# State space outputs transposed and in pairs of heads, decays in two rounded parts, feed-forward weights rounded transposed

## The reference

```python
zxbcdt = u @ W_in
z, xBC, dt = split(zxbcdt, [1024, 1024 + 1280])
conv = conv_b + sum over 4 taps of shifted xBC * conv_w[i]
x, B, C = split(silu(conv), [1024, 1152])       # 16 heads of 64; state 128
dt = softplus(dt + dt_bias);  A = -exp(A_log)
y, _ = ssd(x * dt, A * dt, B, C)                # y[l] = sum over s <= l of (C[l].B[s]) exp(sum of A dt over s+1..l) x[s] dt[s]
y = (y + x * D) * silu(z)
y = y * rsqrt(mean(y * y) + eps) * norm_scale
out = y @ W_out
# feed-forward, weights and activations rounded to 255 steps per row (scale = max|row| / 127)
gate, up = split(quant(h) @ quant(w_gate_up).T);  out = quant(silu(gate) * up) @ quant(w_down).T
```

## Time and profile before

| | |
|---|---|
| median of 3 runs | 1077.93 us (1075.56 to 1081.33) |
| the profiled execution | 1079.65 us, of which its span (first to last instruction) 1077.9 us |
| busy in the span | PE 95%, DVE 68%, ACT 53%, POOL 25% |
| mean granted TensorE clock | 0.988 of full |

### The profile page before, as it was taken

One profiled execution on the slowest core, in us unless ns is written; L12 is line 12 of the kernel. 1 busy time (PEld: TensorE's weight loads), 2 busy tenths in 40 slices (PEclk: granted clock), 3 DMA queues, 4 the chain that ended last, 5 costly groups with the idle time before them and its releaser, 6 DMA issues.

```text
span 1077.9 us, 18635 instructions
## 1 busy us (share of the span) xinstructions
PE 1020.7 (95%) x6849; PEld 809.4 (75%) x6849; DVE 734.0 (68%) x1441; ACT 572.2 (53%) x1227; POOL 269.1 (25%) x209
## 2 busy tenths in 40 slices
PE   8989989999998899999999999999999999898996
PEld 5545789999996666687888878787877879667743
DVE  3656455556644889788887878888788876554534
ACT  3345344444434210677767677776767769343413
POOL 6810144444332200022220212222022011104411
PEclk9999999999999999999999999999999999999998
DMA  9450075566623232111020211202021126404010
GB/s 276 113 237 1 13 252 207 209 211 216 226 72 100 86 101 81 48 30 33 8 77 4 54 33 31 57 5 71 13 61 42 42 65 148 143 6 161 1 64 20
DMA packets 72253, 97.49 MB, mean 90 GB/s; under 512 B 35665, under 2 KB 53233, under 8 KB 71026
## 3 DMA queue, kind: packets, MB, share of 16 engines
q1 hardware_dynamic: 72178, 96.49, 28.6%
HBM read 91.58 MB, written 4.90 MB: 89 GB/s over the span
## 4 chain that ended last, share of the span: by engine, by line
PE 79%; DVE 12%; ACT 5%; issue 2%; DMA 1%; POOL 1%; SPq 0%; DVEq 0%; ACTq 0%; POOLq 0%
PE PS L1551 16%; PE PS L1424 12%; PE PS L1540 10%; PE PS L1528 8%; PE PS L1443 5%; PE PS L1513 4%; DVE scores L1078 2%; PE PS L1565 2%; PE PS L1272 2%; PE PS L1637 2%; ACT scores L788 1%; PE PS L1720 1%; PE PS L1646 1%; PE PS L1324 1%; PE PS L1483 1%
## 5 line engine op out<-in xcount | busy, mean ns | idle before, releaser
L1133 DVE TENSOR_TENSOR pL<-PS,pH 128x512 fp32r<-128x512 f32 x256 | 175.9, 687 | 60.1 <-ACT pH L812 59.2
L812 ACT ACTIVATE pH<-PS 128x512 fp32r<-128x512 f32 x256 | 151.7, 595 | 100.4 <-PE PS L1540 100.4
L788 ACT ACTIVATE scores<-scores,nmX 128x512 f32<-128x512 f32 x256 | 185.1, 723 | 18.5 <-DVE nmX L1082 18.5
L1078 DVE TENSOR_SCALAR_CACHE_REDUCE scores<-PS 128x512 f32<-128x512 f32 x256 | 172.6, 682 | 20.4 <-PE PS L1528 20.2
L1551 PE MATMUL PS<-pH,kvH 128*128 128x256 f32 x512 | 164.5, 321 | 6.6 <-ACT xnT L797 6.6
L1540 PE MATMUL PS<-ident,scores 128*128 128x128 f32 x1024 | 157.1, 276 | 1.0 <-DVE pL L1133 1.0
L1551 PE MATMUL PS<-pL,kvH 128*128 128x256 f32 x512 | 144.0, 281 | 0.0
L1551 PE MATMUL PS<-pH,kvL 128*128 128x256 f32 x512 | 143.7, 281 | 0.0
L1540 PEld LDWEIGHTS PS<-ident,scores 128*128 128x128 f32 x1024 | 117.3, 140 | 32.0 <-issue 14.4
L1551 PEld LDWEIGHTS PS<-pH,kvH 128*128 128x128 f32 x512 | 96.7, 189 | 10.8 <-issue 10.6
L1551 PEld LDWEIGHTS PS<-pL,kvH 128*128 128x128 f32 x512 | 97.2, 190 | 0.0
(11 more groups left out here) (309 smaller groups left out, 2273.9 us busy)
## 6 DMA issues: line engine op xcount, KB each, us to landing
rawG<-in_wg SPq DMA_DIRECT2D x16, 768.0 KB, 5.7
rawU<-in_wu SPq DMA_DIRECT2D x16, 768.0 KB, 7.1
rawD<-in_wd SPq DMA_DIRECT2D x16, 768.0 KB, 6.1
xn<-in_w SPq DMA_DIRECT2D x11, 512.0 KB, 3.7
wblk<-blocks SPq DMA_DIRECT2D x4, 1056.0 KB, 8.1
wb<-w_rows SPq DMA_DIRECT2D x32, 128.0 KB, 3.3
wqX<-in_wqX SPq DMA_DIRECT2D x16, 256.0 KB, 2.6
woX<-in_woX SPq DMA_DIRECT2D x8, 512.0 KB, 4.8
```

Of the source, the lines that this page charges most:

```text
L788: act.activation(at, at, ACT.Exp, bias=nmX[:, p % 2, h, q:q + 1], accum_out=csum[:, p % 2, NT * h + q, c:c + 1]).then_inc(exp_done, 1)
L812: act.activation(pH[:, i % 4], PS[:, 2 + i % 2, :].rearrange("p (k t) -> p k t", t=T), ACT.Copy).then_inc(pH_ready, 1)
L1078: dve.tensor_scalar(sp_[:, h, q, c * CH:(c + 1) * CH], PS[:, 4 * q + h, :], 1.0, None, ALU.mult, ALU.max, accum_out=cmax[:, h, q, c:c + 1] ...
L1133: dve.tensor_tensor(pL[:, i % 4], PS[:, 2 + i % 2, :].rearrange("p (k t) -> p k t", t=T), pH[:, i % 4].bitcast(F32), ALU.subtract).then_in ...
```

## The change

Feed-forward weights: DRAM inputs `w1t` and `w2t` hold the weights turned; the rows are still read for their maxima (`w2` first), scales and their inverses go to DRAM (`s_rows`, `i_rows`), the inverses come back spread over all partitions (`winvB`), and POOL rounds turned pieces of 1024 columns, 17 jobs, of which slots 4 to 8 hold two each (`round_columns`). They are stored turned and loaded straight to `wturned`, behind `wout`, with no wait for z. The blocks' transposes and copies are gone.

State space: z is projected transposed too, in four pairs of 128-channel groups (`z_pair`), two of them ahead of the transposes, one between `log_decay(0)` and `log_decay(1)`, one behind. B and C come first of the ten groups. A step is now a pair of heads `m` (8 steps): `ua` holds masked decays as moving operand in two parts, `avH` rounded (fp32r) and the rest `avL`, six pairs deep, made on POOL in four instructions a pair; `log_decay` has six fp32r products; one Exp and one mask multiply of 768 columns a pair; `ssm_out` puts the two heads' outputs, channels x tokens, in the two column halves. DVE adds x D from PSUM (`yt`) and multiplies by silu(z) (`yz`), which is the stationary operand of `project`, done per pair inside the loop. POOL multiplies `wout` by `norm_scale` and adds up the squares. All `stay_awake` calls ahead of the output projection's end in this part are gone.

```diff
+TURN1, TURN2 = GT // 2, (FT + 1) // 2
+TURNED_AT = {DT - 1: [(2, 0)]}
+for job in range(TURN1):
+    TURNED_AT[DT + job] = [(1, job)] + ([(2, job + 1)] if job + 1 < TURN2 else [])
+TURNED = [job for slot in sorted(TURNED_AT) for job in TURNED_AT[slot]]
+TURNED_STORED = [0]
+for kind, job in TURNED:
+    TURNED_STORED.append(TURNED_STORED[-1] + 16)
+UA = 6
+XORDER = (CT // 2 - 1,) + tuple(range(CT // 2 - 1))
...
+        zs = A("zs", [P, IT, T]); xdt = A("xdt", [P, NT, DI]); yt = A("yt", [P, 2, T]); yz = A("yz", [P, IT, T])
...
+        avH, avL = (A(n, [P, NT, SH], F32R) for n in ("avH", "avL"))
+        after = A("after", [P, P]); upto = A("upto", [P, T]); ones = A("ones", [P, P])
+        afterR, onesR = (A(n, [P, P], F32R) for n in ("afterR", "onesR"))
+        ua = A("ua", [P, UA, 2, 6 * P], F32R)
+        gm = A("gm", [P, 6 * P]); decay = A("decay", [P, 2, 6 * P]); mh = A("mh", [P, 2, 6 * P])
...
+            def rows_and_columns(n):
+                sp.wait_ge(winv_ready, n + 1)
+                store_scales(n)
+                if n + 1 < JOBS:
+                    load_rows(n + 1)
+                for kind, job in TURNED_AT.get(n, ()):
+                    k = TURNED.index((kind, job))
+                    if k:
+                        sp.wait_ge(wint_ready, k)
+                        store_turned(*TURNED[k - 1])
+                    sp.wait_ge(scale_stored, STORED[n + 1])
+                    load_turned(kind, job)
...
-            sp.wait_ge(ssm_pe.sem, ssm_pe.at("z", NT))
             for part in range(4):
-                e = slice(part * BLOCKS // 4, (part + 1) * BLOCKS // 4)
-                sp.dma_start(wblk[:, e], blocks[:, e]).then_inc(wblk_in, 16)
+                e = slice(part * BLOCKS // 4 * P, (part + 1) * BLOCKS // 4 * P)
+                sp.dma_start(wturned[:, e], turned[:, e]).then_inc(wturned_in, 16)
...
+            def round_columns(k):
+
+                kind, n = TURNED[k]
...
+                pool.wait_ge(wcol_in, 32 * (k + 1))
+                step(pool.tensor_tensor(part.rearrange("p (k o) -> p k o", o=shape[2]), part.rearrange("p (k o) -> p k o", o=shape[2]), inverse, ALU.mult))
+                step(pool.tensor_tensor(part, part, constant, ALU.add))
+                wait(pool, wint_stored, TURNED_STORED[k])
+                pool.tensor_tensor(wint[:, 0:cols], part, constant, ALU.subtract).then_inc(wint_ready, 1)
...
+            def weighted(m):
+                h2 = slice(2 * m, 2 * m + 2)
+                wait(pool, d_ps, m - UA + 1)
+                for j, part in enumerate((avH, avL)):
+                    pool.tensor_tensor(ua[:, m % UA, j, 0:2 * T].rearrange("p (h l) -> p h l", h=2), upto[:].unsqueeze(1).broadcast_to([P, 2, T]),
+                                       part[:, 0, h2].bitcast(F32).unsqueeze(2).broadcast_to([P, 2, T]), ALU.mult)
+                    ins = pool.tensor_tensor(ua[:, m % UA, j, 2 * T:].rearrange("p (h l) -> p h l", h=2), upto[:, 0:P].unsqueeze(1).broadcast_to([P, 2, P]),
+                                             part[:, 1, h2].bitcast(F32).unsqueeze(2).broadcast_to([P, 2, P]), ALU.mult)
+                ins.then_inc(ua_ready, 1)
+
+            for m in range(IT // 2):
+                weighted(m)
+            pool.wait_ge(wout_in, 16)
+            pool.wait_ge(ssm_in, 96)
+            for m in range(IT):
+                pool.tensor_tensor(wout[:, m, :], wout[:, m, :], ns[:, m:m + 1].broadcast_to([P, D]), ALU.mult).then_inc(wout_ready, 1)
+            for m in range(IT // 2, IT):
+                weighted(m)
+            for m in range(IT - 1):
+                pool.wait_ge(yz_ready, m + 1)
+                if m == 0:
+                    step(pool.tensor_tensor(y2s[:], yz[:, m], yz[:, m], ALU.mult))
+                else:
+                    step(pool.tensor_tensor(y2[:], yz[:, m], yz[:, m], ALU.mult))
+                    step(pool.tensor_tensor(y2s[:], y2s[:], y2[:], ALU.add))
+            pool.sem_inc(y2_ready, 1)
...
+            for k, m in enumerate(XORDER):
+                act.wait_ge(ssm_pe.sem, ssm_pe.at("xbc", k + 1))
+                act.activation(xp[:, 2 * m:2 * m + 2, CONV - 1:], PS[:, k, :].rearrange("p (c t) -> p c t", t=T), ACT.Copy).then_inc(xp_ready, 1)
+                act.wait_ge(xp_ready, k + 1)
                 for c in (2 * m, 2 * m + 1):
                     act.activation(cv[:, c], xp[:, c, 0:T], ACT.Identity, bias=cb[:, c:c + 1], scale=cw[:, c, 0:1]).then_inc(ssm_act.sem, 1)
+                if k:
+                    silu_pair(k - 1)
+            silu_z(0)
+            silu_pair(CT // 2 - 1)
+            silu_z(1)
+
+            def exp_pair(m):
+                b = m % 2
+                bank = 2 if b else 6
+                act.wait_ge(d_ps, m + 1)
+                wait(act, mh_ready, m - 1)
+                act.activation(decay[:, b], PS[:, bank:bank + 2, :].rearrange("p b n -> p (b n)")[:, 0:6 * P], ACT.Exp).then_inc(decay_ready, 1)
+
+            exp_pair(0)
+            for j in range(2):
+                act.wait_ge(z_ps, 3 + j)
+                act.activation(zs[:, 4 + 2 * j:6 + 2 * j], PS[:, 1 - j, :].rearrange("p (c t) -> p c t", t=T), ACT.Copy).then_inc(zs_ready, 1)
+                if j == 0:
+                    exp_pair(1)
+            exp_pair(2)
+            exp_pair(3)
+            act.wait_ge(zs_ready, 4)
+            act.activation(zs[:, 4:8], zs[:, 4:8], ACT.Silu).then_inc(zs_ready, 2)
+            for m in range(4, IT):
+                exp_pair(m)
+            act.wait_ge(yz_ready, IT)
+            act.activation(y2l[:], yz[:, IT - 1], ACT.Square).then_inc(late_act.sem, 1)
...
+            for t in range(NT):
+                dve.wait_ge(ssm_pe.sem, ssm_pe.at("xsT", t + 1))
+                dve.tensor_tensor(xdt[:, t].rearrange("p (h c) -> p h c", c=HP), PS[:, 2 + 2 * t:4 + 2 * t, :].rearrange("p b (h c) -> p (b h) c", c=HP),
+                                  dtv[:, t].unsqueeze(2).broadcast_to([P, SH, HP]), ALU.mult).then_inc(ssm_dve.sem, 1)
+            step(dve.tensor_tensor(gm[:, 0:2 * T].rearrange("p (h l) -> p h l", h=2), PS[:, 0, 0:T].unsqueeze(1).broadcast_to([P, 2, T]),
+                                   upto[:].unsqueeze(1).broadcast_to([P, 2, T]), ALU.mult))
+            step(dve.tensor_tensor(gm[:, 2 * T:].rearrange("p (h l) -> p h l", h=2), PS[:, 0, T:T + P].unsqueeze(1).broadcast_to([P, 2, P]),
+                                   upto[:, 0:P].unsqueeze(1).broadcast_to([P, 2, P]), ALU.mult))
+            dve.sem_inc(ssm_dve.sem, 1)
+
+            def masked(m):
+                dve.wait_ge(decay_ready, m + 1)
+                wait(dve, y_ps, m - 1)
+                dve.tensor_tensor(mh[:, m % 2], decay[:, m % 2], gm[:], ALU.mult).then_inc(mh_ready, 1)
+
+            masked(0)
+            masked(1)
+            for m in range(IT):
+                dve.wait_ge(y_ps, m + 1)
+                step(dve.scalar_tensor_tensor(yt[:, m % 2], act_[:, m], dskip[:, m:m + 1], PS[:, 4 + m % 2, 0:T], ALU.mult, ALU.add))
+                if m + 2 < IT:
+                    masked(m + 2)
+                dve.wait_ge(zs_ready, m // 2 + 1 if m < 4 else 6)
+                dve.tensor_tensor(yz[:, m], yt[:, m % 2], zs[:, m], ALU.mult).then_inc(yz_ready, 1)
...
+            def z_pair(j, bank):
+                for c in (2 * j, 2 * j + 1):
+                    for kt in range(KT):
+                        mm = pe.matmul(PS[:, bank, (c % 2) * T:(c % 2 + 1) * T], win[:, kt, c * P:(c + 1) * P], xnT[:, kt, :],
+                                       start=(kt == 0), stop=(kt == KT - 1))
+                mm.then_inc(z_ps, 1)
+
+            z_pair(0, 6)
+            z_pair(1, 7)
             pe.wait_ge(xp_ready, CT // 2)
             pe.wait_ge(ssm_dve.sem, ssm_dve.at("a", 1))
+            pe.wait_ge(ssm_act.sem, ssm_act.at("silu4", 2))
             for t in range(NT):
                 for m in range(IT):
                     mm = pe.transpose(PS[:, 2 + 2 * t + m // 4, (m % 4) * P:(m % 4 + 1) * P], act_[:, m, t * P:(t + 1) * P], ident[:])
                 mm.then_inc(ssm_pe.sem, 1)
+            pe.matmul(PS[:, 0, 0:T], act_[:, IT, 0:P], act_[:, IT + 1, :], start=True, stop=True)
+            pe.matmul(PS[:, 0, T:T + P], act_[:, IT, P:T], act_[:, IT + 1, P:T], start=True, stop=True).then_inc(ssm_pe.sem, 1)
+            pe.wait_ge(ssm_consts, 5)
+
+            def log_decay(m):
+                bank = 2 if m % 2 else 6
+                pe.wait_ge(ua_ready, m + 1)
+                wait(pe, decay_ready, m - 1)
+                for j in range(2):
+                    pe.matmul(PS[:, bank, :], afterR[:], ua[:, m % UA, j, 0:2 * T], start=(j == 0), stop=False)
+                for j in range(2):
+                    pe.matmul(PS[:, bank, :].rearrange("p (h l) -> p h l", h=2)[:, :, P:T], onesR[:], ua[:, m % UA, j, 2 * T:].rearrange("p (h l) -> p h l", h=2),
+                              start=False, stop=(j == 1))
+                for j in range(2):
```

(57 more changed lines are left out.)

274 lines of the change are left out of this document (84 added, 190 removed).

## The result

The changed kernel takes 1109.38 us (median of 4 runs, 1098.67 to 1114.06), the kernel before 1077.97 (4 runs, 1075.56 to 1081.33). The ratio is 1.0275, with a 95% interval of 1.019 to 1.036: slower by 31 us, where 6.5 us less were forecast. The profiled run of the changed kernel is its fastest, 1098.67 us with a span of 1096.9.

A forecast was written before the change was run, and what follows sets the result against it. TensorE, busy for 95% of the span, was taken to bound the kernel. An output projection ending 7.5 us earlier, less 1 us for the loop's clock, took 6.5 off the median 1077.93: 1071.4 us, range 1056 to 1080.

The forecast's parts named there:

- cross-attention term: Cross-attention stage: reordered rounding and SP's extra small stores, column loads and waits cost 0 us, from -1 to +3.
- Rival D: Cross-attention eats A's gain through a late slice of `win`, or ACT and DVE held: 6 us, 1077; chance 0.10.
- Taps held by POOL: Convolution on DVE: taps alternate with POOL's operations, 1.0 us on average where they were 0.47, ending at 977.
- Clock behind the idle stretch: PE after standing still for 12 us before the loop: lowered clock loses 1.9 us.
- Circle: Head-pair loop: `project`, `log_decay`, Exp, mask, `yz` and four handovers set 5.1 us per pair, PE waiting for `yz`.
- rival C: Head loop: gaps keep the clock at its lower level, six circles of 2.7 us more, 1086; chance 0.12.
- the microsecond set aside for it: Head loop: 1 us taken as likeliest loss to a lower clock, with 0 to 16 as bounds.
- End of the output product: Output projection ends 36.6 us after the loop's start, at 1027.7, 7.5 us earlier than 1035.2.
- Last slice of `win`: End of cross-attention: slice leaves near 924, lands near 932, 5 us before PE needs it at 937.
- The sum: Whole kernel: 7.5 - 1 = 6.5 us less, taken off the median 1077.93, gives 1071.4.
- rival A: The forecast itself: convolution taps are held by POOL; 1071.4 us, own range 1065 to 1078; chance 0.60.

The follow-up runs named there:

- e3: Changed kernel without any small stores of scales and inverses or waits for them, output not the reference's; 1070.39 us.
- e11: Kernel before the change, with GpSimd's inverse scales also stored as 128 pieces of 4 bytes that nobody reads; 1099.28 us.
- e1: Changed kernel without the stores of the inverse scales; broadcast loads read the scales instead, so the stored integers are wrong; 1073.57 us.
- e4: Changed kernel with the load of the next job's rows issued ahead of the four small stores; 1092.95 us.
- e8: e3 with GpSimd's weighted decays and scalings of wout begun only when VectorE's taps are done; 1068.06 us.
- e7: e3 with yz(m) ahead of masked(m+2) on VectorE in the head-pair loop; 1059.74 us.
- e6: Changed kernel with scale columns transposed on VectorE, each store 4 pieces of 128 bytes instead of 128 of 4; 1074.29 us.
- e9: Changed kernel with the edits of e6, e7 and e8, and wout scaled on ScalarE instead of GpSimd; 1053.81 us.

## Why the prediction was wrong, point by point

The step that failed is the cross-attention term: "I take 0, with -1 to +3." It is +25.8 us in the profiled run, and with e3, where the small stores are gone, it is 0 (a stage of 485.1 us for 485.4). The sentence ahead of it lists "more small stores, column loads and waits" on SP's queue, and prices only who waits for what. The transfers themselves got no price, and the number of their pieces was not read at all. Two stores a slot were harmless before, which made a third and fourth look so too; e11 prices them by themselves at 22 us, e1 shows that up to two cost little (2.7 us of the stage), and e3 that nothing else in the stage costs. What they did is in no term of the sum: PE's signals to ACT were up to 7.2 us late (e4).

Rival D had the right place and the wrong cause and size: 6 us for "a late slice of `win`, or ACT and DVE held by the new order". ACT was held, and DVE behind it, but not by the new order: in e11 it is the order of before. Four times that was lost.

The median of the changed kernel lies 10.7 us above its profiled run, the fastest of the four. No trace of the slower ones exists, so this part of the 31 us isn't explained.

The rest, less the shift of 25.8 us:

- Taps held by POOL: forecast an end at 977 and 1.0 us each; measured 976.3 and 1.02. e8 confirms the cause by taking it away. The Trainium skill, SBUF — State Buffer, section "Who interferes with whom", has a DVE instruction with two SBUF inputs contend with a GpSimd one that reads SBUF; the taps, 1.02 us beside POOL and 0.47 alone, agree.
- Clock behind the idle stretch: 1.9 us forecast; the transposes alone took 1.7 more, and from 1000 to 1010 us the granted clock was 0.65 on average.
- Circle: 5.1 forecast, 5.26 measured, and e7 shows that the order of `yz` and `masked` is what closes it. The loop ran at a clock of 1.00, so rival C, with 0.12, and the microsecond set aside for it were not needed.
- End of the output product: 1027.7 forecast before that microsecond, 1028.4 measured. The 42.7 us behind it are unchanged.
- Last slice of `win`: issued near 924 by the forecast; it was issued 26 us later, and in e1, with half of the small stores, at 921.26.
- The sum: e3, the change without small stores, takes 1070.4 for the 1071.4 forecast.

So rival A's mechanism was right in its terms for the state space part, and another place decided the time. That e3 comes within 1 us of 1071.4 rests on its parts and hardly on luck: the loop took 0.7 us more than forecast, which the unneeded microsecond for the clock covers.

## What to carry to other kernels

Count the pieces of every transfer that a change adds, not its bytes: a [128, 1] column to memory is 128 pieces of 4 bytes, and four of them in a row cost 22 us here where nothing else was changed (e11). Turn such a column into rows of 32 on DVE first (e6), and keep what an in-order engine consumes ahead of the small stores. When an engine stands idle though the product that it needs has ended, look at what the DMA queues were doing, and at when the signal rose, before you blame its instructions; and compare stages by marks inside one trace, since their entry alone may wander by 8 us.

## What the runs showed of the hardware

- Four stores of 128 pieces of 4 bytes took 16.5 us from the first issue to the end of the wait (e6: four pieces of 128 bytes each, 3.1). For six such microseconds, in e4, the DMA engines were idle but for three small packets. Two in a slot: SP waits 7.3 us at most (e1). The Trainium skill, DMA: Bandwidth & Descriptors, section "Why small descriptors are slow (HBM only)", names a fixed cost for each piece; the direction agrees (16.5 us for 512 pieces, 3.1 for 16), and no run here shows that cost by itself.
- With four such stores under way, PE's signals to other engines came up to 7.2 us after the end of their product, several then within 0.4 us, and ACT stood idle for up to 7.01 us. The Trainium skill, Runtime: NRT & Kernel Launch, section "Instruction fetch mechanics", calls the cost of fetching instructions mostly hidden; the traces agree so far as packets stretched to 3.0 us in the kernel before held no engine.
- Two-input operations of DVE and POOL alternate one by one for 30 us, and each is held by the other: taps take 1.02 us for 0.47, POOL's `ua` of 256 elements 0.79 for the 0.61 that it takes alone in e9.
- PE was idle from 991 to 1003 us. From 1000 to 1010 the granted clock was 0.65 on average, which lies between its two levels of 1.2 and 2.4 GHz; in the loop, with PE busy for 7.4 of 10 us in clumps, it was 1.00.
